# Attention numerators, denominators and inverses loaded head by head in 16-row transfers; the experts' slots zeroed in five portions

## What is computed

```python
x = x + attn_causal(attn_prior(x))     # two attentions, 16 heads of 16 channels each
x = x + ffn(mixer(x))                  # 8 experts of 320 slots, top 2, plus a shared expert
```

```python
attn = softmax(scores, axis=-1)        # = p / p.sum()
y = einsum('bhqk,bhkd->bhqd', attn, v) # 16 channels per head
```

## Time and profile before

| | |
|---|---|
| median of 3 runs | 1787.53 us (1787.46 to 1789.6) |
| the profiled execution's own time | 1797.83 us |
| its span in the profile | 1796.0 us |
| PE busy (matmul) | 1625.0 us, 90% |
| DVE, ACT, POOL busy | 919.1, 742.1, 645.0 us |
| granted TensorE clock, mean | 0.94 of full speed |
| DMA queue of SP and its share of 16 engines | 68987 packets, 113.61 MB, 22.2% |

### The profile page before, as it was taken

How to read it: one execution, slowest core, us unless ns; L and a number is a source line. 1 busy time by engine, 2 the same in 40 slices (tenths; PEclk the granted TensorE clock), 3 DMA queues, 4 the chain that set the end, 5 groups by cost and what they waited for, 6 DMA issues and landing times.

```text
span 1796.0 us, 20631 instructions
## 1 busy us (share of the span) xinstructions
PE 1625.0 (90%) x7632; PEld 771.4 (43%) x7632; DVE 919.1 (51%) x2045; ACT 742.1 (41%) x1028; POOL 645.0 (36%) x353
## 2 busy tenths in 40 slices
PE   5789899778989988887899988999999999999998
PEld 3433223223322322433343323545655566666655
DVE  6679688898658866445665552225312111111131
ACT  4744555455555555365555557233221111111111
POOL 5437889876788989031000000220001100000051
PEclk9569999999999999998899988999999999999999
DMA  3450213313131220244231002300030004233052
GB/s 103 141 140 24 60 33 86 88 44 83 44 78 33 67 48 7 72 123 145 74 74 42 22 22 83 119 15 0 0 141 6 19 1 169 86 128 128 14 103 39
DMA packets 72737, 121.42 MB, mean 68 GB/s; under 512 B 12009, under 2 KB 50354, under 8 KB 69308
## 3 DMA queue, kind: packets, MB, share of 16 engines
q1 hardware_dynamic: 68987, 113.61, 22.2%
q0 software_dynamic: 3072, 6.03, 1.9%
q10 hardware_dynamic: 576, 0.47, 0.1%
HBM read 85.08 MB, written 36.96 MB: 68 GB/s over the span
## 4 chain that ended last, share of the span: by engine, by line
PE 48%; DVE 5%; DMA 4%; ACT 4%; SPq 2%; POOL 2%; issue 2%; another core or an unknown queue 1%; ACTq 0%; DVEq 0%; POOLq 0%
PE wide L1962 19%; PE wide L1974 5%; PE wide L1980 5%; PE wide L1903 4%; PE wide L1880 3%; PE bank L1753 3%; DMA sb_den<-o_raw 2%; POOL sb_prob L1085 2%; PE bank L1852 2%; DVE sb_rowmax L1558 1%; ACT sb_prob L1287 1%; PE wide L1852 1%; DMA sb_xg<-slots_in 1%; PE bank L1745 1%; PE wide L1885 1%
## 5 line engine op out<-in xcount | busy, mean ns | idle before, releaser
L1085 POOL TENSOR_TENSOR sb_prob<-sb_prob,sb_weight 128x1024 f32<-128x1024 f32 x192 | 453.4, 2385 | 111.2 <-ACT sb_prob L1287 110.4
L1287 ACT ACTIVATE sb_prob<-wide 128x1024 f32<-128x1024 f32 (+3 forms) x384 | 348.5, 917 | 279.2 <-PE wide L1885 154.5
L1880 PE MATMUL wide<-sb_stack_q,sb_stack_k 99*128 99x512 bf16 (+3 forms) x896 | 299.0, 373 | 27.2 <-DVE sb_prob L1617 19.1
L1852 PE MATMUL bank<-sb_stack_k,sb_stack_q 96*128 96x512 bf16 (+3 forms) x596 | 220.3, 388 | 53.1 <-DVE sb_rowmax L1558 28.7
L1564 DVE CUSTOM_DVE_ANT_0 sb_junk<-bank,sb_bias 128x512 bf16<-128x512 f32 x339 | 225.8, 686 | 72.0 <-PE bank L1852 69.3
L1331 ACT ACTIVATE sb_sil<-wide 128x320 f32<-128x320 f32 (+1 forms) x128 | 66.2, 517 | 459.6 <-PE wide L1962 419.6
L1903 PE MATMUL wide<-sb_prob,sb_v_aug 128*17 128x512 f32 (+3 forms) x1792 | 231.1, 580 | 17.6 <-POOL sb_prob L1085 9.6
L1962 PE MATMUL wide<-sb_weight,sb_ffn 128*128 128x512 f32 x512 | 233.0, 598 | 0.0
L1709 DVE TENSOR_TENSOR sb_act_s<-sb_sil,wide 128x512 f32<-128x512 f32 x64 | 43.9, 686 | 268.3 <-ACT sb_sil L1331 242.4
L1558 DVE TENSOR_REDUCE sb_rowmax<-bank 128x1 f32<-128x512 f32 (+3 forms) x257 | 136.3, 553 | 74.0 <-PE bank L1855 41.6
L1962 PE MATMUL wide<-sb_xgT,sb_big 128*128 128x320 f32 x512 | 152.8, 444 | 1.1 <-ACT sb_xgT L1346 1.1
(11 more groups left out here) (258 smaller groups left out, 1946.4 us busy)
## 6 DMA issues: line engine op xcount, KB each, us to landing
sb_stack_k<-parts SPq DMA_DIRECT2D x32, 256.0 KB, 6.9
o_raw<-sb_o_raw SPq DMA_DIRECT2D x32, 256.0 KB, 2.2
sb_big<-rg SPq DMA_DIRECT2D x8, 1024.0 KB, 5.0
sb_big<-ru SPq DMA_DIRECT2D x8, 1024.0 KB, 7.1
sb_big<-rd SPq DMA_DIRECT2D x8, 1024.0 KB, 9.8
sb_stack_q<-parts SPq DMA_DIRECT2D x16, 384.0 KB, 5.0
parts<-sb_o_norm SPq DMA_DIRECT2D x48, 128.0 KB
sb_stack_q<-parts SPq DMA_DIRECT2D x16, 256.0 KB, 5.4
```

The source lines that it names most:

```text
L1085: e.tensor_tensor(p, p, weight_of(*u[1:]), ALU.mult).then_inc(weigh_p.handle, 1)
L1287: e.activation(p[:, :, first:HALF], sc[:, :, first:HALF], ACT.Exp).then_inc(SC.empty_sem(u), 1)
L1852: i = e.matmul(bk[:, 0:hi - lo], stack_q[0:ROWS, n % 3, h, qt * P:(qt + 1) * P], stack_k[0:ROWS, n % 3, h, lo:hi], start=True, stop=not diag)
L1880: i = e.matmul(sc[:, j * HALF + first:(j + 1) * HALF], stack_k[0:ROWS_M, n % 3, g, kt * P:(kt + 1) * P], stack_q[0:ROWS_M, n % 3, g, half ...
```

## The change

The loads of a pair are cut up by head: where `num` had two transfers of 64 rows of numerators and two of 64 rows of denominators, it has eight of 16 rows each, and all eight denominators go first. The inverse is loaded by eight transfers of 16 rows instead of one of 128. The zeroing after job 9 becomes five portions of 512 slots after jobs 9, 10, 11, 12 and 13; the cleared piece of SBUF is half as large. The sizes moved are the same. The waits count all eight transfers.

```diff
@@ -44,6 +44,7 @@
 I_R, I_S = 4 * D, 8 * D
 CAP = max(int(1.25 * T / E), 1)
 SLOTS = E * CAP
+ZEROED = 5
 TILES = [(0, P), (P, P), (2 * P, CAP - 2 * P)]
 PAIRS_OF = QUAD // 2
 LEAD = 0.6
@@ -396,7 +397,9 @@
         if (att, b, q) == (1, 0, 0):
             plan.append(("mixload",))
         if (att, b, q) == (1, 0, 1):
-            plan += [("woload",), ("zero",)]
+            plan.append(("woload",))
+        if causal and n - len(JOBS) // 2 in range(1, 1 + ZEROED):
+            plan.append(("zero", n - len(JOBS) // 2 - 1))
         if q == NQ - 1 and n + 1 < len(JOBS):
             extras += GAP + outputs(att, b)
             if att == 0:
@@ -620,7 +623,7 @@
         first = o_norm[:, 0].bitcast(BF16)
         late_parts = [(first[:, 2 * k * HALF:(2 * k + 1) * HALF], first[:, (2 * k + 1) * HALF:(2 * k + 2) * HALF],
                        tabs[:, k * HALF:(k + 1) * HALF]) for k in range(2)]
-        zeros = unlisted[:, NT // 2:].rearrange("p a t -> p (a t)").bitcast(F32)
+        zeros = unlisted[:, NT // 2:].rearrange("p a t -> p (a t)").bitcast(F32)[:, 0:SLOTS // ZEROED * D // P]
         spare = unlisted[:, 0:2].rearrange("p a t -> p (a t)").bitcast(F32)
         idle = [z.bitcast(BF16)[:, k * HALF:(k + 1) * HALF] for z in (prob[:, 4], prob[:, 5], spare, y1[:, 0], y1[:, 1])
                 for k in range(2 * S // HALF)]
@@ -693,7 +696,7 @@
         load = {k: signal(f"load_{k}", range(n), 16) for k, n in dict(
             cb=1, idx=3, ones=3, cf=2, x0=2, x1=2, w1=1, w2=1, wo=1, small=3, mix=13, wproj=1).items()}
         ffn_in = [signal(f"load_ffn{k}", ["sg", "su", "sd"], 16) for k in range(BLOCKS)]
-        zero_done = signal("zero_slots", range(4), 16)
+        zero_done = signal("zero_slots", range(ZEROED + 1), 16)
         count_kq_done = signal("count_kq_stored", range(NT), 16)
         count_qk_done = [signal(f"count_qk_stored{k}", TURNS[k::ROW_BUFS], 16) for k in range(ROW_BUFS)]
         PRODUCTS = {ab: [u for u in of("product") if u[1:3] == ab] for ab in ((0, 0), (0, 1), (1, 0), (1, 1))}
@@ -710,10 +713,10 @@
                      for k in range(2)]
         PAIRS = [u[1:] for u in of("num")]
         o_out = [signal(f"store_o{half}", range(len(JOBS)), 16) for half in range(NH)]
-        num_in = [signal(f"load_num{c}", [(*u, par) for u in PAIRS if u[2] == c for par in range(2)], 16) for c in range(DC)]
-        den_in = signal("load_den", [(*u, par) for u in PAIRS for par in range(2)], 16)
+        num_in = [signal(f"load_num{c}", [(*u, h) for u in PAIRS if u[2] == c for h in range(2 * QUAD)], 16) for c in range(DC)]
+        den_in = signal("load_den", [(*u, h) for u in PAIRS for h in range(2 * QUAD)], 16)
         inv_out = signal("store_inverse", PAIRS, 16)
-        inv_in = signal("load_inverse", PAIRS, 16)
+        inv_in = signal("load_inverse", [(*u, h) for u in PAIRS for h in range(2 * QUAD)], 16)
         inv_done = signal("dve_inverse", PAIRS)
         times_p = signal("pool_times", PAIRS)
         scaled = signal("pool_scale", ["b0", "b1"])
@@ -869,19 +872,21 @@
                         w.wait_ge(BK.filled(OUTS[PAIRS[k - DC][0:2]][-1]))
                     if c and (att, b) != (1, 1):
                         w.wait_ge(split_p.after(("third", *PRODUCTS[((0, 1), (1, 0), (1, 1))[k // DC]][-1][1:])))
-                    for par in range(2):
-                        src = o_d[2 * k % 4 + par].rearrange("(h r) t -> h r t", r=HB)
-                        half_rows = slice(par * P // 2, (par + 1) * P // 2)
-                        e.dma_start(o_norm[half_rows, c], src[:, 0:DH]).then_inc(num_in[c].handle, 16)
-                        e.dma_start(den[half_rows], src[:, DH].rearrange("h (a t) -> h a t", a=DH)
-                                    ).then_inc(den_in.handle, 16)
+                    heads = [(slice(h * DH, (h + 1) * DH), o_d[2 * k % 4 + h // QUAD][h % QUAD * HB:(h % QUAD + 1) * HB])
+                             for h in range(2 * QUAD)]
+                    for rows, src in heads:
+                        e.dma_start(den[rows], src[DH].rearrange("(a t) -> a t", a=DH)).then_inc(den_in.handle, 16)
+                    for rows, src in heads:
+                        e.dma_start(o_norm[rows, c], src[0:DH]).then_inc(num_in[c].handle, 16)
                 elif kind == "inv":
                     w.wait_ge(inv_done.after(u[1:]))
                     e.dma_start(inv_dram.rearrange("h (a t) -> (h a) t", a=DH), den[:]).then_inc(inv_out.handle, 16)
                     w.wait_ge(inv_out.after(u[1:]))
                     if PAIRS.index(u[1:]):
                         w.wait_ge(times_p.after(PAIRS[PAIRS.index(u[1:]) - 1]))
-                    e.dma_start(inv_b, inv_dram.unsqueeze(1).broadcast_to([2 * QUAD, DH, S])).then_inc(inv_in.handle, 16)
+                    for h in range(2 * QUAD):
+                        e.dma_start(inv_b[h * DH:(h + 1) * DH], inv_dram[h:h + 1].broadcast_to([DH, S])
+                                    ).then_inc(inv_in.handle, 16)
 
             for u in ATT:
                 kind = u[0]
@@ -933,11 +938,11 @@
                     fetch_in("cf", cf[:, P:P + 2 * E], A["const_f32"][:, CF["iota_e"][0]:CF["iota_e"][0] + 2 * E])
                 elif kind == "zero":
                     w.wait_ge(zeroed.end)
-                    for o in range(0, SLOTS, P * S * DC // D):
-                        n = min(P * S * DC // D, SLOTS - o)
-                        e.dma_start(slots_in[o:o + n, :].rearrange("(p k) n -> p (k n)", p=P),
-                                    zeros[:, 0:n * D // P]).then_inc(zero_done.handle, 16)
-                    e.dma_start(slots_out[SLOTS:SLOTS + 1, :], zeros[0:1, 0:D]).then_inc(zero_done.handle, 16)
+                    n = SLOTS // ZEROED
+                    e.dma_start(slots_in[u[1] * n:(u[1] + 1) * n, :].rearrange("(p k) n -> p (k n)", p=P),
+                                zeros).then_inc(zero_done.handle, 16)
+                    if u[1] == 0:
+                        e.dma_start(slots_out[SLOTS:SLOTS + 1, :], zeros[0:1, 0:D]).then_inc(zero_done.handle, 16)
                 elif kind == "kb_load":
                     _, b, t = u
                     for mark in parts_stored(0, 1):
@@ -972,8 +977,8 @@
                     cols = slice(half * HALF, (half + 1) * HALF)
                     if n >= 4:
                         was = PAIRS[n // 2 - 2]
-                        w.wait_ge(num_in[was[2]].after((*was, 1)))
-                        w.wait_ge(den_in.after((*was, 1)))
+                        w.wait_ge(num_in[was[2]].after((*was, 2 * QUAD - 1)))
+                        w.wait_ge(den_in.after((*was, 2 * QUAD - 1)))
                     w.wait_ge(PV.emptied((n, half)))
                     e.dma_start(o_d[n % 4][:, cols], o_raw[:, 0, cols]).then_inc(o_out[half].handle, 16)
                 elif kind == "w2load":
@@ -1054,8 +1059,8 @@
                 e.tensor_scalar(bcol[:, 2 * att], bcol[:, 2 * att], SCALE, None, ALU.mult).then_inc(scaled.handle, 1)
 
             def times(u):
-                w.wait_ge(num_in[u[3]].after((*u[1:], 1)))
-                w.wait_ge(inv_in.after(u[1:]))
+                w.wait_ge(num_in[u[3]].after((*u[1:], 2 * QUAD - 1)))
+                w.wait_ge(inv_in.after((*u[1:], 2 * QUAD - 1)))
                 e.tensor_tensor(o_norm[:, u[3]], o_norm[:, u[3]], inv_b, ALU.mult).then_inc(times_p.handle, 1)
 
             for u in ATT:
@@ -1073,7 +1078,7 @@
                     w.wait_ge(listed_a.after(u[1:]))
                     w.wait_ge(tables_a.after(("kw", *u[1:])))
                     e.tensor_tensor(o, o, listed_w[t % 2], ALU.add).then_inc(weight_p.handle, 1)
-                elif u[0] == "zero":
+                elif u == ("zero", 0):
                     w.wait_ge(SC.emptied([v for v in of("score") if JOBS[v[1]][0] == 0][-1]))
                     e.memset(zeros, 0.0).then_inc(zeroed.handle, 1)
                 elif u[0] == "times":
@@ -1508,7 +1513,7 @@
                     w.wait_ge(stat_a.after(u))
                     e.reciprocal(rms[:, ts], rms[:, ts]).then_inc(sl, 1)
                 elif kind == "inv":
-                    w.wait_ge(den_in.after((*u[1:], 1)))
+                    w.wait_ge(den_in.after((*u[1:], 2 * QUAD - 1)))
                     e.reciprocal(den[:], den[:]).then_inc(inv_done.handle, 1)
                 elif kind == "resid":
                     _, b, mc, half = u
```

## The result

The changed kernel ran in 1773.5 us, the median of 4 runs (1768.3 to 1774.8), beside 1788.6 for the kernel before in the same comparison (4 runs, 1787.5 to 1794.2). The two medians lie 15.1 us apart. The ratio of the comparison, which is not the quotient of these medians, is 0.9889, with a 95% interval from 0.9864 to 0.9914; of 1790 us that is 19.9 us less. A second comparison of the same kernel gave 0.9880 (0.9846 to 0.9915), 21.5 us, with medians of 1771.1 and 1791.2, 20.1 us apart. Three of the four runs of before in the first comparison are those of the prediction's 1787.53; the wider sets of the later comparisons (9 to 23 runs) have medians of 1791.1 to 1795.3. The profiled execution took 1773.2 us (span 1771.4) against 1797.8 (1796.0): 24.6 less.

The account below looks back on a forecast made before the run. DVE's waits for denominators, and PE's waits behind them, were taken as the bound. PE's gain of 21.0 us plus 3.6 us of clock made 24.6, from a median of 1787.5 to 1763 us; range 1752 to 1780.

Parts of the forecast that it names:

- What bounds the kernel: DVE waits 23.7 us for denominators at pairs 1, 3, 4, 5, queued behind 512 KB of numerators on four DMA engines.
- The denominators at pair 3: Eight 16-row issues take 3.7 us, denominators land at about 732.4, 6 us before the old 738.3; DVE's wait goes.
- Pair 4: After job 9, one portion of zeros instead of 2.6 MB ahead: DVE waits 0.9 us instead of 11.88.
- the first sign of my list: What would show the forecast right: DVE's waits for `den` total under 3 us.
- PE's gain: PE's four waits for row maxima, 21.9 us together, shrink to 0.9, a gain of 21.0 us.
- POOL's `times` releases PE at pair 3: Sign of being wrong: PE's first `y` matmul at pair 3 would wait for POOL's product; forecast no wait, nothing to spare.
- The inverse's load: Eight 16-row loads take 5.1 to 5.6 us against 6.93, at a DMA share of 6 to 9 tenths; no gain added.
- The clock: PE's granted clock rises in the stretches after the four waits: bounds 0 and 7.1 us, the middle, 3.6, taken.
- Waits that move: Rival: engines come sooner to the next late thing; half of PE's gain and no clock, 10.5 us, 1777. Chance 20%.
- A fixed delay of the denominators: Rival: small pieces need their 11.74 us from issue whatever else runs, so the time is 1788. Chance 6%.
- SP as the bound: Rival: issues on SP take up to 1.35 us each, `times` ends late at pairs 3, 5, 7: 1808. Chance 6%.
- A serial price for each transfer: Rival: 24 small transfers pass one after another at 1.46 us each, `times` ends near 764: about 1808. Chance 3%.

Follow-up runs that it names:

- order alone: The kernel before with a pair's two 64-row denominator loads ahead of its two numerator loads, no 16-row transfers or portions: 1780.6 us, ratio 0.9927.
- stacks behind: The changed kernel with the stack loads that stood ahead of pairs 0 to 5 moved behind the pair's numerators: 1781.2 us, ratio 0.9939.
- portions alone: The kernel before with only the zeroing changed, into five portions: 1787.0 us, ratio 0.9976.
- inverse-alone kernel: The kernel before with only the inverse's load changed, into eight 16-row transfers: 1793.2 us, ratio 1.0003.
- its repeat: The changed kernel run again without an edit, among the follow-up runs: 1771.1 us, ratio 0.9880.
- denominators early: The changed kernel with pair 3's stack loads behind the inverse's load, and denominators ahead of zeros and stack loads at pairs 4 and 5: 1772.9 us, ratio 0.9889.
- The last kernel: The kernel before with 64-row denominator loads first and the zeroing in five portions, no 16-row transfers: 1770.2 us, ratio 0.9869.

## Why the prediction was right, and where it was off

**What bounds the kernel: right.** The DVE waits for denominators were the path, and the numerators' 512 KB on few DMA engines were what held them at pairs 1 and 5 (order alone). At pairs 3 and 4 the stack loads and the zeros had their share as the prediction said (stacks behind: wait 0; portions alone: 11.88 to 6.17 us).

**The denominators at pair 3: the term was too large.** Forecast: the last of eight leaves 3.2 us after the pair's start, lands 7.6 after it, no wait. Measured: 4.05 (one issue took 1.29 us with the queues full) and 9.7, a wait of 1.61 us. The landing behind the stack loads was the error: 5.66 us from the last issue, not 4.4. At pairs 1 and 5 the wait went as forecast, but for 0.55 us. The portion of zeros ahead of pair 5, which the text had at 1.3 us, cost 1.4 us of waiting where nothing else was changed (2.85 to 4.21 us, portions alone).

**Pair 4: 2.96 us left where 0.9 was forecast.** SP's part came out (4.5 us from the zeroing to the pair instead of 9.8; forecast 5), and again the landing behind the stack loads did not: the first sign of my list, under 3 us of DVE waits for `den`, failed with 5.1.

**PE's gain: 18.0 us for 21.0.** 21.9 less the 3.9 left. Of this the product at pair 3 took back 0.75 (0.6 more than in the kernel before); the text had "nothing to spare" there and kept up to 4 us for the range. The first `y` matmul before and after:

```profile
749.92 1.96 PE L1745 MATMUL wide<-sb_o_norm,sb_w_o 128*128 128x512 f32 x4 [0.16 <-POOL sb_o_norm L1059]
```

```profile
733.02 1.96 PE L1750 MATMUL wide<-sb_o_norm,sb_w_o 128*128 128x512 f32 x4 [0.75 <-POOL sb_o_norm L1064]
```

"POOL's `times` releases PE at pair 3" was on the list of signs of being wrong. It happened, at a price of 0.75 us. It had also happened before, after 0.16 us, which the text overlooked. The inverse's load was right, 5.3 us from its first issue to the release of POOL (5.1 to 5.6 forecast), though the share of 6 to 9 tenths that I had announced for it was not: it ran at 4 to 6. Probably SP, which issues 64 KB every 0.46 us, is the limit there; no run varied that. With the numerators narrow, that missing slack is what costs the order-alone kernel 4.15 us.

**The clock: 3.6 us was about half.** The stages that hold the waits became 24.2 us shorter, 6.9 more than the 17.3 of PE's waits. Some 2.9 of them lie at pair 1, 0.9 at pairs 3 and 4 and 3.1 at pair 5. The text had priced these places at 0.9, 4.8 and 1.5 us for a full clock, taken half, and left the stretch behind 450 us out. Pair 1 can be taken apart. The stage from pair 1 to 2 of the kernel before, of the portions alone and of the order alone, columns as in the earlier trace rows:

```profile
433.26:599.42 166.16, 151.53 (x702) 52.28 (x701) 114.19 (x292) 88.55 (x107) 133.03 (x66) 0.94 0.23 58
```

```profile
428.81:595.08 166.27, 151.87 (x702) 52.11 (x701) 114.16 (x292) 88.52 (x107) 133.03 (x66) 0.94 0.23 58
```

```profile
425.32:584.69 159.37, 147.65 (x702) 51.40 (x701) 114.02 (x292) 88.60 (x107) 133.05 (x66) 0.97 0.24 60
```

The same 702 matmuls are recorded in all three. The first two keep the wait and have a clock of 0.94; the third has lost it and has 0.97. Its stage is 6.8 us shorter: PE was idle for 2.9 us less and busy for 3.9 us less. So the clock gave back more than the idle time here. The other profiles agree: this stage took 166.1 to 166.3 us in the three that wait over 3 us at pair 1, and 158.3 to 160.1 in the eleven that do not. (The change's own stage shows 147.4 us of PE with 12 records fewer, and is not used.) At pair 5 nothing so clear can be said: the inverse-alone kernel kept its wait of 3.09 us there and still had a stage of 107.1 us with a clock of 0.98, against 110.2 and 0.95 before. The 3.1 us may be a difference between executions.

**The sum in the end.** Profile against profile the forecast of 24.6 us is met to the tenth, and that is luck: 3.7 us too much for waits (21.0 for 17.3), 3.3 too little behind them (3.6 for 6.9), and 0.4 left of the first and the last stage (4.1 gained, 3.7 lost), which also differ by as much between kernels that are equal there. The two comparisons give 19.9 and 21.5 us, so some 3 to 5 us of the 24.6 are not in the ratios. That is about what the choice of the profiled executions explains: before's took 1797.8 us, 6.7 above the 1791.1 that its wider sets of runs have as median, and the change's 1773.2, 2.2 above the 1771.1 of its repeat. The forecast of 1763 missed the median of 1773.5 by 10 us. Some 4 of them come from its base, 1787.5, the median of three executions, against those 1791.1; the rest from the gain, which was smaller than 24.6.

**The rivals.** Waits that move: in the change only the 0.75 us for the product; it was the right account of what comes next (stacks behind, denominators early). A fixed delay of the denominators: refuted by the order alone. The remark with it, that the order alone would free them and the time be my forecast, held for the denominators, and for the time only once the zeros were in portions as well. SP as the bound: the 24 loads of a pair were issued in some 0.46 us each, but for one or two of 1.0 to 1.7 us at each of the pairs 2 to 7. That is above the 0.8 us of my list for single issues, and nowhere for a whole pair. The 32 loads of 8 rows cost some 5 us by the ratio, not the 20 of the rival. A serial price for each transfer: refuted, the last of 16 loads was in 9.4 us after the pair's start, issued between 0 and 8.2 us and with the stack loads beside them. No rival brought the kernel to the slower side.

The rule that I read from the Trainium skill, page "DMA: Bandwidth & Descriptors", section "Why a DMA increments its semaphore by 16 and not by 1", agrees with the views as far as they go: 4 heads ran at 2 tenths in the order-alone kernel, and the 16-row loads show no such stretch. That these use all 16 engines is not seen by itself, since the numerators' rest ran at 4 and 5 tenths. The other, in its section "Rules for kernel authors", to coalesce small transfers, spoke against the change, and the change was faster. The last kernel shows it half right: with the zeroing in portions the same time is to be had with 5 transfers a pair instead of 24. Without the portions the small ones were 6.0 us ahead.

## What to carry to other kernels

When an engine waits for a small load, look at the DMA share during the wait. A long stretch at a fraction of the engines, like the 2 tenths here, can mean that something narrow is in front; put the small load ahead of it before you reshape anything. Then ask for whom the thing that is now behind is late (here the inverse's store, and the product): the order alone and the stack loads behind each left PE with a wait of 4 to 7 us for the product. A wait taken away can also give back more than its own length, through the clock behind it (3.4 us of PE's waiting at pair 1 brought 6.8). And hold a profile's difference against several runs: executions of equal code differ here by 3 to 6 us in single stages.

## What the hardware showed that I had not expected

- A store of 32 KB took 1.46 us on free DMA engines, 4.51 us with narrow numerators in flight and 6.91 us behind 1.5 MB of stack loads: in these three cases its time went with what stood in front of it.
- The granted clock was 0.82 in a stretch in which PE was busy for all of 20 us, and 1.00 in the same stretch of another execution of the same kernel. The stages around such a place differ by 3 to 6 us (142.8 and 146.1 between pairs 0 and 1 in the change's repeat and with the denominators early, which issue the same instructions up to there; 125.4 and 128.4; 661.6 and 667.4).
- SP's issues became no dearer with their number: 0.46 us for a 16-row load, 0.35 to 0.39 for an 8-row one. Single ones of 1.0 to 1.7 us stand in the loads of pairs 2 to 7 of the change, at pair 3 (1.29 us) right behind the stack loads. What makes them slow was not looked at.
